# Two products of the layer-1 head moved from VectorE to GpSimd, and every engine's order written anew

## What is computed

```python
x = L0_attn_x                                   # (4, 1024, 256)
xn = _layernorm(x)
s = _L0_attn_ref(xn, ...)                       # wavelets, linear attention, layer norm
g = _silu(_L0_ffn_ref(xn, ...))                 # ternary matrices 256 -> 1024 -> 1024 -> 1024 -> 256
x = x + s * g
xn = _layernorm(x)
s = _L1_attn_ref(xn, ...)                       # selective state space model, 16 states, and an FFN
g = _silu(_L1_ffn_ref(xn, ...))                 # 8 experts, the best two of each token
x = x + s * g
```

```python
xn = layernorm(x, ln1_g, ln1_b)
delta = softplus(xn @ Wd.T + bd)
Bm, Cm = xn @ Wbc.T + bbc                       # split in two, 16 states each
h = exp(delta * A) * h + delta * Bm * xn        # one step for each token and state
y = sum over states of h * Cm
ssm_out = x + y + D * xn
```

## Time and profile before

| | |
|---|---|
| median of 3 runs | 1765.97 us (1763.22 to 1766.5) |
| profiled execution | 1762.41 us, of it span 1760.5 us |
| busy share of the span | PE 82%, DVE 75%, ACT 69%, POOL 56% |
| mean granted clock of PE | 0.916 of full speed |
| chain that ended last | PE 43%, DVE 21%, ACT 17%, issue 12%, POOL 7% |

### The profile page before, as it was taken

The page is one execution under the profiler, slowest core; times in us unless marked ns, Lnnn a source line. Parts: engine busy times, 40 slices in busy tenths (PEclk is TensorE's granted clock), DMA queues, the critical chain, the costliest instruction groups (busy, mean ns, idle before and its releaser), DMA issues.

```text
span 1760.5 us, 16736 instructions
## 1 busy us (share of the span) xinstructions
PE 1449.7 (82%) x5296; PEld 629.0 (36%) x5296; DVE 1317.6 (75%) x1610; ACT 1216.7 (69%) x1699; POOL 977.6 (56%) x616
## 2 busy tenths in 40 slices
PE   3979989899898789899898789899998763565687
PEld 1434444444443334444443234434443221112232
DVE  1663369899685689989785679989785679887943
ACT  3626779777639879767638779868539864675576
POOL 2143165766008885766108786756207873785665
PEclk9989999899999999999999899999999875777889
DMA  8010000000201000000201000000100300000000
GB/s 196 7 36 24 1 12 1 25 1 1 84 0 36 24 25 1 24 1 1 84 1 36 25 24 1 24 1 1 72 13 8 125 24 0 0 1 0 1 12 12
DMA packets 12601, 42.45 MB, mean 24 GB/s; under 512 B 1866, under 2 KB 1890, under 8 KB 10466
## 3 DMA queue, kind: packets, MB, share of 16 engines
q1 hardware_dynamic: 11698, 35.08, 5.4%
q0 software_dynamic: 816, 6.30, 1.6%
HBM read 38.23 MB, written 4.19 MB: 24 GB/s over the span
## 4 chain that ended last, share of the span: by engine, by line
PE 43%; DVE 21%; ACT 17%; issue 12%; POOL 7%; DMA 0%; POOLq 0%; DVEq 0%; SPq 0%; ACTq 0%
PE psf L1510 7%; DVE st L2243 6%; PE psy L1682 5%; PE psu L1697 4%; DVE psu L2226 3%; PE psu L1799 3%; PE psy L1775 2%; PE psf L1399 2%; PE psy L1460 2%; PE psf L1460 2%; ACT da L1103 2%; POOL ap L797 2%; PE psu L1775 2%; PE psu L1399 2%; PE psy L1535 2%
## 5 line engine op out<-in xcount | busy, mean ns | idle before, releaser
L769 POOL TENSOR_TENSOR gx<-gx,sy 128x1024 f32<-128x1024 f32 x120 | 286.9, 2391 | 93.8 <-DVE sy L2259 88.7
L792 POOL TENSOR_TENSOR gate<-gate,lin 128x512 f32<-128x512 f32 x120 | 156.5, 1317 | 293.8 <-DVE gate L2375 270.1
L1510 PE MATMUL psf<-g1p,h2w 128*128 128x512 f16 x768 | 180.6, 383 | 2.4 <-ACT tf L972 2.4
L2226 DVE TENSOR_TENSOR psu<-so,psu 128x1024 f32<-128x1024 f32 x128 | 156.3, 1221 | 26.4 <-PE psu L1635 25.1
L752 POOL TENSOR_TENSOR g2p<-tf,g2p 128x512 fp32r<-128x512 f32 x64 | 95.7, 1502 | 140.4 <-ACT g2p L995 140.4
L1103 ACT ACTIVATE da<-delta,aneg 128x512 f32<-128x512 f32 x256 | 164.7, 710 | 12.8 <-DVE st L2243 9.4
L2243 DVE TENSOR_TENSOR_SCAN st<-da,carry,psu 128x512 f32<-128x512 f32 x128 | 156.8, 1266 | 1.8
L2243 DVE TENSOR_TENSOR_SCAN st<-da,psu 128x512 f32<-128x512 f32 x128 | 149.1, 1206 | 1.7
L797 POOL TENSOR_TENSOR ap<-gate,ap 128x512 f16<-128x512 f32 x116 | 138.7, 1212 | 19.9 <-ACT ap L1208 19.9
L2259 DVE TENSOR_TENSOR sy<-st,psu 128x1024 f32<-128x1024 f32 x94 | 114.5, 1218 | 11.4 <-issue 5.7
L1510 PE MATMUL psf<-hp,h1w 128*128 128x512 f16 x512 | 117.5, 379 | 0.0
(11 more groups left out here) (396 smaller groups left out, 3381.2 us busy)
## 6 DMA issues: line engine op xcount, KB each, us to landing
mw<-in_mlp_w SPq DMA_DIRECT2D x3, 2048.0 KB, 8.0
...
```

Source lines behind the costliest of these rows:

```text
L769: pool.tensor_tensor(out, chunk(gx, c), sy[:, n % 2], ALU.add).then_inc(y_acc.sem, 1)
L792: pool.tensor_tensor(gate[:, r % NG], gate[:, r % NG], lin_at(b, r)[:], ALU.mult)\
L1510: last = pe.matmul(banks[m], w[:, t, cols], src[:, half, t], start=(t == 0 and half == 0), stop=(t == KF - 1 and half == 1))
L2226: dve.tensor_tensor(input_banks(n), chunk(so, c), both(psu[:, row_bank(n)]), ALU.mult)\
```

## The change

POOL gets the first product of `head_norm` for all eight heads (`head_scale`), and the last product for chunk 0 too (`head_product(b, c)`). On DVE `head_norm` is one instruction, which now waits for POOL's product, and `head_last` is gone. The orders of POOL, ACT, PE and DVE are written anew in `opening`, `turn` and `closing`; the set of all other instructions is the same, but for one ACT table load more. Of the new orders the diff shows the lines on the moved products and on the gate:

```diff
 
-            def head_product(b):
-
-                pool.wait_ge(le_step.sem, le_step.at(b, NC * LE_STEPS))
-                pool.tensor_tensor(chunk(so, 1), delta[1][:], xn1(b, 1), ALU.mult).then_inc(head_done.sem, 1)
+            def head_scale(b, c):
+
+                pool.wait_ge(le_rstd.sem, le_rstd.at(b, 2 * c + 1))
+                if c == 0 and b > 0:
+
+                    pool.wait_ge(x2n.sem, x2n.at(b, NC))
+                pool.tensor_tensor(xn1(b, c), xc[c], both(delta[c][:, 1]), ALU.mult).then_inc(le_step.sem, 1)
+
+            def head_product(b, c):
+
+                pool.wait_ge(le_step.sem, le_step.at(b, (c + 1) * LE_STEPS))
+                pool.tensor_tensor(chunk(so, c), delta[c][:], xn1(b, c), ALU.mult).then_inc(head_done.sem, 1)
 
             def l0_product(b, c, w):
...
-                l0_product(0, 0, wave0); l0_out(0, 0, wave0); ffn_task(0, 1, 16); ffn_task(0, 1, 17)
-                ffn_task(0, 1, 18); ffn_task(0, 1, 19); ffn_task(0, 1, 20); ffn_task(0, 1, 21); ffn_task(0, 1, 22)
-                l0_low(1, 0); ffn_task(0, 1, 23); l0_product(0, 1, wave0); l0_out(0, 1, wave0)
+                l0_product(0, 0, wave0); l0_out(0, 0, wave0); head_scale(0, 0); ffn_task(0, 1, 16); ffn_task(0, 1, 17)
+                ffn_task(0, 1, 18); ffn_task(0, 1, 19); ffn_task(0, 1, 20); ffn_task(0, 1, 21); head_product(0, 0)
+                ffn_task(0, 1, 22); l0_low(1, 0); ffn_task(0, 1, 23); l0_product(0, 1, wave0); l0_out(0, 1, wave0)
...
-                state_product(row - 1, 0, 4); state_add(row - 1, 0, 4); state_add(row - 1, 0, 5)
-                state_product(row - 1, 0, 6); state_add(row - 1, 0, 6); state_add(row - 1, 0, 7)
...
+                ffn_task(row, 0, 6); ffn_task(row, 0, 7); state_add(row - 1, 0, 2); state_product(row - 1, 0, 4)
+                state_add(row - 1, 0, 3); state_add(row - 1, 0, 4); state_product(row - 1, 0, 6)
+                state_add(row - 1, 0, 5); state_add(row - 1, 0, 6); head_scale(row - 1, 1)
...
+                l0_low(row, 1); state_add(row - 1, 0, 12); state_add(row - 1, 0, 13); ffn_task(row, 0, 21)
+                head_product(row - 1, 1); ffn_task(row, 0, 22); ffn_task(row, 0, 23); state_add(row - 1, 0, 14)
...
+                head_scale(row, 0); expert_low(row - 1, 15); expert_product(row - 1, 17); expert_low(row - 1, 16)
...
+                head_product(row, 0); expert_low(row - 1, 28); expert_low(row - 1, 29); expert_low(row - 1, 30)
...
-                state_product(b, 0, 1); state_add(b, 0, 0); state_add(b, 0, 1); state_add(b, 0, 2)
-                state_product(b, 0, 3); state_add(b, 0, 3); state_product(b, 0, 5); state_add(b, 0, 4)
+                state_add(b, 0, 0); state_product(b, 0, 1); state_add(b, 0, 1); state_add(b, 0, 2); head_scale(b, 1)
+                state_product(b, 0, 3); state_add(b, 0, 3); state_add(b, 0, 4); state_product(b, 0, 5)
...
-                carry_state(row - 1, 15); decay(row - 1, 19); l0_gate(row, 0); ffn_task(row, 1, 0)
+                ffn_task(row, 1, 0); l0_gate(row, 0); ffn_task(row, 1, 1); ffn_high(row, 1, 0); ffn_high(row, 1, 1)
...
             def head_norm(b, c):
 
-                dve.wait_ge(le_rstd.sem, le_rstd.at(b, 2 * c + 1))
-                if c == 0 and b > 0:
-
-                    dve.wait_ge(x2n.sem, x2n.at(b, NC))
-                yield from head_step(b, c, 1, dve.tensor_tensor(xn1(b, c), xc[c], both(delta[c][:, 1]), ALU.mult))
+                dve.wait_ge(le_step.sem, le_step.at(b, LE_STEPS * c + 1))
                 dve.wait_ge(le_rstd.sem, le_rstd.at(b, 2 * c + 2))
-                yield from head_step(b, c, 2, dve.tensor_tensor(xc[c], xc[c], both(hb(b, c)), ALU.mult))
+                dve.tensor_tensor(xc[c], xc[c], both(hb(b, c)), ALU.mult).then_inc(le_step.sem, 1)
 
...
-            def head_last(b, c):
-
-                dve.wait_ge(le_step.sem, le_step.at(b, LE_STEPS * (c + 1)))
-                dve.tensor_tensor(chunk(so, c), delta[c][:], xn1(b, c), ALU.mult).then_inc(head_done.sem, 1)
 
...
-                state_scan(row - 1, 0, 7); ffn_task(row, 0, 12); ffn_task(row, 0, 13); run(norm1)
-                state_output(row - 1, 0, 7); run(norm1); state_input(row - 1, 0, 8); state_scan(row - 1, 0, 8)
+                state_input(row - 1, 0, 7); state_scan(row - 1, 0, 7); state_output(row - 1, 0, 7)
+                ffn_task(row, 0, 12); ffn_task(row, 0, 13); state_input(row - 1, 0, 8); head_norm(row - 1, 1)
...
-                expert_weight(b, 0); state_input(b, 0, 3); run(choice0, 2); state_scan(b, 0, 3); run(choice0, 7)
-                run(norm1); run(choice0, 2); state_output(b, 0, 2); run(choice0, 2); state_input(b, 0, 4)
+                state_input(b, 0, 3); run(choice0, 2); state_scan(b, 0, 3); run(choice0, 11); state_output(b, 0, 2)
```

753 lines of the change are left out of this document (375 added, 378 removed).

## The result

The changed kernel takes 1740.28 us (median of 4 runs, 1739.28 to 1742.14) against 1765.87 for the kernel before (4 runs): a ratio of 0.9859, 95% interval 0.9842 to 0.9876, 25.6 us faster. I had predicted 1761.0 and a range from 1751 to 1773: the gain is five times what I forecast, and outside the range. The profiled execution took 1739.98 us, span 1738.2, with a mean granted clock of 0.931 (0.916 before); the two profiled executions lie 22.4 us apart.

What follows compares the result with a forecast made beforehand. The prediction took one chain through four engines, mostly on PE, as the bound. A turn's +0.3 - 1.0 - 2.0 + 1.7 = -1.0, three turns -3, closing -2, together -5, gave 1761.0 us, range 1751 to 1773.

Steps and rivals of the forecast that it cites:

- State stage, +0.3: Head of chunk 1: DVE waits at its second product for POOL's `head_scale`; +0.3 us in each of three turns.
- the high bound: State stage, +2.4 us: the two `g1p` could be held up by one POOL instruction more.
- Gate, -1.0: Gate of layer 0: table load moves ahead of the wait, so the gate starts 1.0 us earlier in each turn.
- Convolution stage, -2.0: Hidden block fills PE's idle before the logits, keys' product follows them directly; -2.0 us a turn.
- the 1 us that I named: Expected sign in the changed profile: PE has under 1 us idle before the convolution stage's logits.
- Expert stage, +1.7: `head_scale` costs nothing; `head_product` on POOL delays the last four `expert_low`, less some relief; +1.7 us a turn.
- the slower case: Whole kernel: both moved products lie on POOL's chain in the expert stage, +4.8 a turn; about 1774 us, chance 0.22.
- that relief: Expert stage: last four `expert_low` take 4.6 us, not 5.92, without DVE's last product; half of that 1.3 counted.
- Closing, -2: Closing: DVE loses 1.14 and a choice-step stall of 2.1, less 1.2 for a new one; bounds -4 and +3.
- the collisions I feared: Closing: `head_scale` on POOL can catch another small DVE instruction, such as the 2.17 at 1469.34; +1.2 us.
- The likeliest case: Whole kernel: a small gain of 3.5 to 9 us, to about 1761; chance 0.36.
- the larger gain: Whole kernel: the reordering pays everywhere, -3.4 us a turn and closing -3; about 1753 us, chance 0.18.

Runs made afterwards that it cites:

- e2: Kernel before with its old orders, the first and last products moved to POOL: 1767.32 us, ratio 1.0016.
- e12: Kernel before with the new order in chunk 0's state stage only, no product moved: 1768.89 us, ratio 1.0019.
- e11: Kernel before with the new order in chunk 0's state stage only, `head_scale` on POOL there: 1772.67 us, ratio 1.0043.
- e8: Kernel before with the new order in the expert stage only, both products left on DVE: 1747.25 us, ratio 0.9896.
- e4: Kernel before with the new order in the expert stage only, its two products moved to POOL: 1753.40 us, ratio 0.9932.
- e1: Changed kernel with all new orders kept but both products back on DVE: 1740.70 us, ratio 0.9861 to the kernel before.
- e9: All new orders except chunk 0's state stage, which stays old, no product moved: 1729.85 us, ratio 0.9807 to the kernel before.
- e10: Changed kernel with chunk 0's state stage old; products of opening, expert stage and closing on POOL: 1729.57 us, ratio 0.9787 to the kernel before.
- e5: Kernel before with one ACT step, the FFN's first with its table load, moved ahead of the gate: 1759.35 us, ratio 0.9962.
- e6: Kernel before with the new order in the convolution stage only: 1758.61 us, ratio 0.9960.
- e3: Kernel before with the new order in chunk 1's state stage only, gate included: 1753.49 us, ratio 0.9937.
- e16: Kernel before with chunk 1's state stage new, but the gate ahead of the FFN's first step as before: 1754.97 us, ratio 0.9945.
- e7: Kernel before with the new order in the closing only, `head_scale` moved there: 1760.92 us, ratio 0.9978.
- e15: All new orders, no product moved, but POOL's order old in chunk 0's state stage: 1738.58 us, ratio 0.9848 to the kernel before.
- e18: Kernel before with the new orders only in the expert stage's second half, no product moved: 1763.61 us, ratio 0.9990.

## Why the prediction was wrong, by its own steps

**The move: a cost, as said, but not of this size.** Sized apart, it costs 2.5 us alone (e2), 3.8 in chunk 0's stage (e12 to e11) and 6.2 in the expert stage (e8 to e4); I had +0.3 and +1.7 a turn, that is 6 in all. In the full new orders it costs nothing measurable: e1 and the changed kernel are equal, and so are e9 and e10. By the traces, the product lengthens the end of the expert stage there, but POOL's wait for `head_late` ahead of it lets DVE through, and the 4.6 us at the start of the next turn are spared. No term or rival of mine had that.

**State stage, +0.3: the step failed, at its mechanism too.** I let DVE wait for POOL at the second product until 292.75. It did not. POOL's times were near (9.9 us from its product to the end of `head_scale`, where I had 9.5), but the delay fell ahead of the second product: on the wait of 1.19 before `sy`, which I had not seen, and on the `g1p` pair, where I had put only the high bound. From POOL's product of state 6 (283.26 before, 282.08 after) to the scan (about 293.8 before, 294.75 after) the changed kernel lost about 2.2 us. And what lay outside of my sum, the rest of the stage's order, costs 4 us over three turns even without the product (e12).

**Gate, -1.0: right in place, too small in price.** Alone it gives 1.7 a turn (e5), and the wait did shrink by 1.07. I priced the wait and not the matmuls behind it, which took 3.60 us where eight at the full clock take 1.90. That row stood in the trace, and in the convolution stage I had used just this argument. In e5 itself the matmuls gave back only 0.7, 0.2 and 0 us, so the rest of its 1.7 lies elsewhere and is not placed.

**Convolution stage, -2.0: right in the sum, partly by luck.** e6 gives 6 us in three turns, but in its trace -0.3, 4.3 and 1.2, not 2 in each. The wait before the logits is 0.79, under the 1 us that I named, and the hidden block of 3.8 is gone, though the rows behind are slower.

**Expert stage, +1.7: near on the two products, wrong on the stage.** Their net cost is 2.0 a turn (e8 to e4), close to 1.7 partly by luck: within the stage it is 2.8 to 4.6, and 4.6 come back once behind it. My sign for the slower case, PE's wait for the last `expert_low` growing by over 3 us, came true (1.06 to 4.94) and misled: with the wait just before it, 3.25 and now 1.32, the two grew by 2.0 together. The last four `expert_low` took 4.49 us (I had 4.6), but so much in the new order of e1 too, so that relief is the order's. The step that failed is the one not taken: I counted the moved products as the stage's whole change, while four orders of 32 blocks were rewritten. That was worth -5.8 a turn (e8).

**Chunk 1's state stage: no term at all** beyond the gate. e3 shows -3.8 a turn; with the gate taken back e16 still has -3.4.

**Closing, -2: e7 shows -4**, inside its bounds. The 2.34 in the choice is gone as said; of the collisions I feared, two of over 2 us in the weights are there.

**The sum.** Stages timed alone without the moves give -17 -11 -6 -4 +4 = -34 (the closing's with its one); together they give -24 (e1). Of the missing 10, 7 lie in chunk 0's stage if the medians are taken as they are (4 alone, 11 among the others), which the intervals don't secure. The other 3 may be gains that overlap, or the opening: its new order is in e1, e9, e10 and e15 and was never timed by itself. The likeliest case and the range both went wrong for one reason: every case, the larger gain too, was built from the places that the diff names, with no term for the rest of the orders. The Trainium skill's rule on the shared port, in "SBUF — State Buffer", section on SBUF's two separate sides, agrees with the pair (2.38 to 4.55 us). It decided 2 to 5 us here and there, in both directions, and not the sign of the whole.

**Open.** Which steps of the expert stage's first half bring its 10 us: one moved function does nothing and ACT's order alone loses, so it takes several engines at once, but which is not separated. Why `head_late` is held in some turns and not in others (in e8 in turns 2 and 3, in e1, e9 and e18 in turns 1 and 2). What the opening's new order is worth. Which of ACT, PE and DVE loses in chunk 0's stage; that wasn't tried.
